# Transposing attention probabilities in row halves, and three moves in the order of VectorE and GpSimd

## The reference

```python
x = layernorm(x + self_attention(x))            # softmax(q k^T / 8) v per head, then w_o
x = layernorm(x + cross_attention(x, ctx))      # attends over heads within one position, not over positions
x = layernorm(x + light_ffn(x) + heavy_ffn(x))  # gelu FFNs 128->64->128 and 128->512->128 on rms-normed x
```

## Time and profile before

| what | us |
|---|---|
| median of 3 executions | 413.41 (412.16 to 416.49) |
| the profiled execution, its own time | 414.85 |
| its span, first to last instruction | 413.0 |
| PE busy / DVE busy / ACT busy / POOL busy | 398.8 / 287.6 / 240.1 / 148.1 |
| mean granted clock of TensorE | 0.994 |

### The profile page before, as it was taken

One profiled execution on the slowest core, in us unless ns is written; L12 is line 12 of the kernel. 1 busy time (PEld: TensorE's weight loads), 2 busy tenths in 40 slices (PEclk: granted clock), 3 DMA queues, 4 the chain that ended last, 5 costly groups with the idle time before them and its releaser, 6 DMA issues.

```text
span 413.0 us, 15941 instructions
## 1 busy us (share of the span) xinstructions
PE 398.8 (97%) x6580; PEld 344.6 (83%) x6580; DVE 287.6 (70%) x661; ACT 240.1 (58%) x813; POOL 148.1 (36%) x224
## 2 busy tenths in 40 slices
PE   8999999999999999999999999999999999798996
PEld 7787888788888888888888898888989888687884
DVE  4686786866848678667757868659566967578445
ACT  5675574745567466655566566457466648336351
POOL 0642434432413454323315444213324445123213
PEclk9999999999999999999999999999999999899999
DMA  7900113110110213100201112200201121102001
GB/s 262 356 5 8 44 26 83 46 32 9 33 23 19 45 32 87 41 14 8 42 13 32 37 41 75 51 2 17 44 8 39 27 49 22 33 12 43 27 26 52
DMA packets 43646, 19.27 MB, mean 47 GB/s; under 512 B 36592, under 2 KB 40944, under 8 KB 43584
## 3 DMA queue, kind: packets, MB, share of 16 engines
q1 hardware_dynamic: 42736, 16.88, 15.8%
q0 software_dynamic: 560, 1.38, 1.0%
q10 hardware_dynamic: 288, 0.07, 0.1%
HBM read 8.88 MB, written 1.05 MB: 24 GB/s over the span
## 4 chain that ended last, share of the span: by engine, by line
PE 83%; DVE 6%; ACT 4%; SPq 3%; issue 2%; DMA 1%; POOL 1%; POOLq 0%; DVEq 0%
PE ps L1151 8%; PE ps L1206 7%; PE ps L1139 7%; PE ps L1063 7%; PE ps L1118 6%; PE ps L1127 6%; PE ps L1035 6%; PE ps L1015 5%; PE ps L1017 4%; PE ps L1016 4%; PE ps L1161 4%; PE ps L1054 3%; SPq L309 3%; PE ps L1145 2%; ACT p L535 2%; PE ps L1094 2%
## 5 line engine op out<-in xcount | busy, mean ns | idle before, releaser
L535 ACT ACTIVATE p<-ps,neg_max 128x128 f32<-128x128 f32 x256 | 90.0, 383 | 42.9 <-DVE neg_max L799 42.9
L406 POOL TENSOR_TENSOR p<-p,row_inv 128x1024 f32<-128x1024 f32 x32 | 60.7, 1896 | 61.7 <-DVE row_inv L805 61.7
L528 ACT ACTIVATE pt<-ps 128x512 f32<-128x512 f32 x62 | 34.5, 625 | 48.7 <-PE ps L1118 48.7
L535 ACT ACTIVATION_READ_ACCUMULATOR p<-ps,neg_max 128x1 f32 x256 | 57.6, 225 | 0.0
L799 DVE TENSOR_REDUCE neg_max<-ps 128x4 f32<-128x512 f32 x64 | 41.5, 671 | 5.6 <-PE ps L1206 4.8
L745 DVE TENSOR_TENSOR ot<-ps,bv 128x512 f32<-128x512 f32 x32 | 22.0, 688 | 30.7 <-PE ps L1139 30.5
L1118 PE MATMUL ps<-ident,p 128*128 128x128 f32 x256 | 34.8, 279 | 1.3 <-POOL p L406 1.3
L1127 PE MATMUL ps<-x1t,wq 128*64 128x64 f32 x1024 | 34.0, 224 | 1.9 <-issue 1.0
L1206 PE MATMUL ps<-kt,qt 64*64 64x128 f32 x1024 | 35.1, 275 | 0.0
L1127 PEld LDWEIGHTS ps<-x1t,wq 128*64 128x64 f32 x1024 | 31.5, 138 | 3.5 <-issue 2.4
L1139 PEld LDWEIGHTS ps<-pt,v 128*64 128x64 f32 x512 | 28.9, 141 | 6.1 <-issue 6.1
(11 more groups left out here) (153 smaller groups left out, 838.1 us busy)
## 6 DMA issues: line engine op xcount, KB each, us to landing
v<-v2s SPq DMA_DIRECT2D x256, 32.0 KB
xg<-x_t SPq DMA_DIRECT2D x4, 256.0 KB, 3.0
pt<-w_qk SPq DMA_DIRECT2D x4, 256.0 KB, 5.1
cg<-ctx_t SPq DMA_DIRECT2D x4, 256.0 KB, 3.6
wo<-w_o SPq DMA_DIRECT2D x2, 512.0 KB, 9.2
xres<-x_nat SPq DMA_DIRECT2D x15, 64.0 KB, 1.7
out<-x2b SPq DMA_DIRECT2D x3, 256.0 KB, 2.3
p<-w_v SPq DMA_DIRECT2D x1, 512.0 KB, 7.0
```

The costliest lines, as they stand in the source:

```text
L406: nc.gpsimd.tensor_tensor(ph, ph, row_inv[:, 8 * half:8 * half + 8].unsqueeze(2).to_broadcast([T, 8, T]), ALU.mult).then_inc(p_ready, 1)
L528: nc.scalar.activation(pt[:, u * BANK:(u + 1) * BANK], bank(T_BANK[u]), ACT.Copy).then_inc(pt_ready, 1)
L535: last = nc.scalar.activation(p[:, hd * T:(hd + 1) * T], bank(S_BANK[q])[:, pos * T:(pos + 1) * T], ACT.Exp, bias=neg_max[:, hd:hd + 1], a ...
```

## The change

`transpose_p` now takes a half (8 heads). Per head it makes two transposes, of query rows 0 to 63 and of rows 64 to 127: a stationary operand of 64 rows by 128 columns and a 64x64 identity streamed through one row half of the array. The upper row half's output goes to one bank and the lower's to the other bank of the half. Both `mm_t` counts come at the end, behind head 7. ACT's copy has as many elements as before, and writes each bank as 8 pieces of 64 columns at a stride of 128 into `pt`. On DVE `inverse_sums(0)` moves from behind `x1_out` to between the two spreadings (or, in step 1, to ahead of `x1_out`), and `regrouped` moves from between the two `q2_out` to ahead of both. On POOL the first normalisation moves ahead of `x1_biased` (L381), to right behind the root.

```diff
+        def pt_part(u):
+            half, e = u // 2, u % 2
+            return (pt[:, half * 8 * T:(half + 1) * 8 * T].rearrange("p (h e q) -> p e h q", h=8, e=2)[:, e],
+                    bank(T_BANK[u]).rearrange("p (h q) -> p h q", h=8))
...
@@ POOL: rstd1 is split, its last part is x1_biased @@
+            def x1_biased(s, b_par):
                 if isinstance(s, int) and s == 1:
                     pool.wait_ge(in_bo2, 16)
                 pool.wait_ge(x1_ready, s)
...
@@ POOL: step; over_sum is the wait for inv_ready and the L406 product @@
-                for half in range(2):
-                    if a:
-                        pool.wait_ge(inv_ready, 2 * s + half + 1)
-                        ...
+                if a:
+                    over_sum(s, 0)
+                if bc:
+                    x1_biased(s, b_par)
+                if a:
+                    over_sum(s, 1)
...
@@ ACT: transposed(u), and the same in the tail @@
-                    nc.scalar.activation(pt[:, u * BANK:(u + 1) * BANK], bank(T_BANK[u]), ACT.Copy).then_inc(pt_ready, 1)
+                    dst, src = pt_part(u)
+                    nc.scalar.activation(dst, src, ACT.Copy).then_inc(pt_ready, 1)
...
@@ DVE: step @@
                     block_diagonal(s, 0)
+                if a and bc:
+                    inverse_sums(0)
+                if d:
                     block_diagonal(s, 1)
                 if bc:
                     x1_out(s)
...
                 if a:
-                    inverse_sums(0)
                     score_max(2)
...
-                    q2_out(s, 0)
                 if d:
                     regrouped(s)
                 if bc:
+                    q2_out(s, 0)
                     q2_out(s, 1)
...
@@ PE @@
-            def transpose_p(n, u):
-                if u % 2 == 0:
-                    pe.wait_ge(p_ready, 2 * n + u // 2 + 1)
-                for i in range(4):
-                    hd = 4 * u + i
-                    last = nc.tensor.transpose(bank(T_BANK[u])[:, i * T:(i + 1) * T], p[:, hd * T:(hd + 1) * T], ident[:])
-                last.then_inc(mm_t, 1)
+            def transpose_p(n, half):
+                pe.wait_ge(p_ready, 2 * n + half + 1)
+                for i in range(8):
+                    hd = 8 * half + i
+                    for e in range(2):
+                        rows = slice(HALF * e, HALF * e + HALF)
+                        mm = nc.tensor.transpose(bank(T_BANK[2 * half + e])[:, i * HALF:(i + 1) * HALF],
+                                                 p[rows, hd * T:(hd + 1) * T], ident[rows, rows])
+                        if i == 7:
+                            mm.then_inc(mm_t, 1)
...
-                    transpose_p(s - 1, 2)
-                    transpose_p(s - 1, 3)
+                    transpose_p(s - 1, 1)
...
                     transpose_p(s, 0)
-                    transpose_p(s, 1)
```

More of the change, by code:

```diff
@@ L387, in rms2, with over_sum @@
                 nc.gpsimd.tensor_tensor(x2b[:, bass.ds((s - 2) * D, D)], x2[:], bdl_row[:], ALU.add).then_inc(x2b_ready, 1)
+            def over_sum(s, half):
+                pool.wait_ge(inv_ready, 2 * s + half + 1)
+                ph = p[:, half * 8 * T:(half + 1) * 8 * T].rearrange("q (h k) -> q h k", h=8)
+                nc.gpsimd.tensor_tensor(ph, ph, row_inv[:, 8 * half:8 * half + 8].unsqueeze(2).to_broadcast([T, 8, T]),
+                                        ALU.mult).then_inc(p_ready, 1)
             def step(s, h, g, phase, a, bc, d):
@@ L400, in step @@
                     rstd1(s, b_par)
-                for half in range(2):
-                    if a:
-                        pool.wait_ge(inv_ready, 2 * s + half + 1)
-                        ph = p[:, half * 8 * T:(half + 1) * 8 * T].rearrange("q (h k) -> q h k", h=8)
-                        nc.gpsimd.tensor_tensor(ph, ph, row_inv[:, 8 * half:8 * half + 8].unsqueeze(2).to_broadcast([T, 8, T]),
-                                                ALU.mult).then_inc(p_ready, 1)
+                if a:
[4 more added lines that the diff above has]
+                    over_sum(s, 1)
                 if d:
@@ L422, in _ @@
             rstd1(B, 1)
+            x1_biased(B, 1)
             minus_max2(LAST)
@@ L1352, in _ @@
                 step(s, s // 2, s // GB, s % GB, s < B, 1 <= s <= B, s >= 2)
-            transpose_p(B - 1, 2)
-            transpose_p(B - 1, 3)
+            transpose_p(B - 1, 1)
             pe.wait_ge(wup_split, 2)
```

## The result

The changed kernel takes 431.21 us (median of 4, 429.78 to 432.15) beside 414.01 us (4, 412.16 to 416.49) for the kernel before: the ratio is 1.042, its 95% interval 1.037 to 1.046. It is 17 us slower where 3.6 us less were forecast. Its profiled execution took 432.15 us, with a span of 430.3. Many lines have new numbers: L1118 is now L1138, L771 is L788, L406 is L401, L1290 is L1311, L1063 is L1082.

The account below looks back on a forecast made before the run. PE, busy 97% of the span, was taken as the bound. Terms +9.0, -3.6, +1.2, -2.0, -1.0, +0.1 and +0.1 gave 3.8 us, taken as 3.6: 413.41 to 409.8 us, range 405.8 to 417.0.

Parts of the forecast that it names:

- its earlier start is worth nothing: POOL's first normalisation, moved ahead of the x1 bias: 1.3 us of spare in most steps, so no gain.
- DVE's reciprocal: Between the spreadings it waits for the last row sum; x1 comes 0.22 us late in nine steps, 2.0 us lost.
- the rivals: Pairs do not gain, 418.8 us (0.13); x1 not late, 407.1 (0.20); path moves off PE, 413.4 (0.15).
- A: Rival on PE's transposes: pairs take 0.109 us and do not gain, 418.8 us; decides from 0.080 a pair; chance 0.13.
- Transposes: On PE, a pair of half transposes takes 0.058 us against 0.109, saving 0.41 us per half on the path.
- The new change of layout: On PE, each half followed by a whole-array block pays 0.19 us; 19 halves, 3.6 us lost.
- The halves' sum: On PE, 22 halves save 9.0 us by shorter transposes, less 3.6 us for new layout changes.
- Regrouping and phase 3: Regrouping first on DVE gains 0.17 us in seven steps, 1.2; three phase 3 steps are 0.35 longer, 1.0 lost.

Follow-up runs that it names:

- the halves alone: Kernel before with only the transposes in row halves and ACT's copies, DVE and POOL in the old order: 411.27 us, ratio 0.994.
- regrouping kept back in phase 3: Kernel before plus halves and the regrouping first, except in phase 3, where it stays between both `q2_out`; reciprocal and POOL as before: 410.1 us, ratio 0.991.
- POOL's product back: Changed kernel with POOL's first normalisation again behind the x1 bias, all else of the change kept: 414.57 us, ratio 1.001 to the kernel before.
- the reciprocal back: Changed kernel with DVE's first reciprocal again behind `x1_out`, POOL keeping its new order: 409.04 us, ratio 0.989 to the kernel before.

## Why the prediction was wrong

**The step that failed** is "its earlier start is worth nothing", of POOL's move, with the `x1_out` of 0.34 us that the step "DVE's reciprocal" took over from the earlier trace rows ("`x1_out` at 236.64, its end 236.98"). Both steps looked at the edits one at a time, and one at a time both are right in kind: POOL's move alone costs nothing, the reciprocal's leaves `x1_out` at 0.34. I never laid the new start of POOL's product beside DVE's list. By the prediction's own figures the reciprocal ended near 236.1 and POOL was free right behind its root, so the product would run from about 236.2 to 238.1, over an `x1_out` at 236.64. The trace of before had the price of such a meeting, in the tail (L731, 0.62 us for 0.34), and I had not read it. Held to the end of the product, x1 would have been 1.4 us late instead of 0.2. Measured are 1.27 us a step, 17.8 us in 14 steps. None of the rivals held it; A, the slower one, stood for another mechanism, which did not come.

**Transposes: right.** A half takes 0.64 us in the chain. With the 0.15 of the earlier trace rows for the change of layout ahead of it a pair takes (0.64 - 0.15)/8 = 0.061 us, for 0.058 forecast. A's limit of 0.080 was not reached.

**The new change of layout: right.** The value projection behind a half takes 0.43 instead of 0.24 us, 0.19 as forecast, and `project_o2` 1.98 in every step but those of phase 3, where block A comes ahead of it and it keeps 1.78.

**The halves' sum: too high.** Forecast were 9.0 - 3.6 = 5.4 us. Between the kernel before and the halves alone, the stretches on PE from the start of a half to the next block shrink by 1.86 us (9 of them, each before a value projection), 1.68 (11, before `project_o2`), 1.14 (3, before L1035) and 0.72 (the rest), together 5.4. That this equals the forecast is chance: in the 1.68 are 1.6 us in which PE now waits for the regrouping. What I had not counted: the first records of the blocks behind are 0.4 us later, and from `project_q2` to the first half it is 1.51 us longer over 15 steps, not evenly but with single steps up to 0.9 longer or 0.8 shorter. The profile has 1.6 us of issue at `project_q2` where it had 1.0; the rest has no cause on record. Measured are 2.8 us by the medians, 2.9 at like clock, so about 0.6 us more stay open.

**Regrouping and phase 3.** The 7 x 0.17 = 1.2 us stand beside 0.75 measured alone, 1.8 at like clock. The chain of before has 1.96 us for `project_o2` also in steps 4 and 12, which the forecast did not count. In phase 3, PE waits 2.7 us ahead of block A in the three steps, but the 0.47 us that its second unit waited are gone. From the half's start to `project_o2` a step takes 4.56 us where it took 4.46: as forecast the half saves nothing there, and the step is 0.1 us longer, or 0.3 with x1's lateness, for 0.35. The run with the regrouping kept back in phase 3 has 4.46 again, so the order alone gives back only this 0.1.

**DVE's reciprocal: the size off.** 2.0 us were counted, for 9 steps and the small rest; measured are 3.3. The mechanism (it waits for the last sum, and the second spreading waits with it) and the delay of a step were right: in the trace with POOL's product back, against the one with the reciprocal back, PE reaches the transpose of x1 later by 2.38 us over 15 steps, and a further 0.5 us comes at the transposes behind. The number of steps was wrong: I had counted nine, and in the reciprocal's move alone the delay is 0.19 us in twelve steps and 0.07 in one.

## What to carry to other kernels

When an edit brings an instruction of GpSimd forward, write down its new interval and every VectorE instruction that begins inside it and works from SBUF to SBUF. A `tensor_scalar` that starts second may last until the other ends, here 1.6 us for 0.34; `bn_stats` was not held, and other instructions are to be looked up in the trace. The meeting may be in the trace already, as one slow member of a group: the longest time of a line beside its median shows it. Two moves that are each free can make such a meeting only together, so the intervals have to be drawn for the whole change, not edit by edit. The cures are cheap: let the short one start first, if only by 0.16 us, cut the long one into pieces, or give the short one an operand in PSUM.

## What the runs showed of the hardware that was not expected

**Hold between DVE and POOL**: a `tensor_scalar` from SBUF to SBUF that starts inside a product of POOL ends 0.08 us behind it, 1.59 against 0.34 us; a product in two pieces (2.04 instead of 1.90 us) lets it in between them; an operand in PSUM frees it (0.40 us). `bn_stats` in SBUF keeps its 0.29 us inside a product. How 0.3 us of work end 0.08 us behind the product's record, no run shows.

**TensorE's clock in the tail.** Behind step 15 PE waits 2.3 to 2.7 us for DVE ahead of the FFN products, and in some executions the granted clock then falls to 0.5 (1.2 GHz) for a time that differs from one execution to the next. The wait alone does not decide it: the third trace below has 2.7 us of it and keeps its clock, the first has 2.3. In three traces (stretch of the span: length, busy us and number of PE, PEld, DVE, ACT, POOL; the granted clock, then DMA), first of the kernel before:

```profile
350.00:354.00 4.00, 3.29 (x83) 2.86 (x81) 2.32 (x7) 1.68 (x4) 1.92 (x3) 1.00 0.24 52
354.00:358.00 4.00, 2.42 (x12) 1.61 (x14) 1.40 (x3) 1.81 (x3) 1.00 (x1) 0.83 0.23 51
358.00:362.00 4.00, 4.00 (x36) 3.61 (x33) 2.16 (x5) 1.15 (x2) 0.32 (x1) 0.74 0.00 0
```

of the run with POOL's product back:

```profile
350.00:354.00 4.00, 1.33 (x26) 1.12 (x19) 2.95 (x6) 1.33 (x3) 1.74 (x3) 0.82 0.23 49
354.00:358.00 4.00, 4.00 (x24) 3.06 (x24) 0.00 (x0) 2.72 (x4) 0.00 (x0) 0.50 0.17 37
358.00:362.00 4.00, 4.00 (x32) 3.57 (x31) 3.15 (x7) 0.60 (x1) 0.62 (x1) 0.83 0.00 0
```

and of the run with the reciprocal back, where the clock stays at full speed:

```profile
350.00:354.00 4.00, 2.78 (x28) 2.27 (x30) 1.11 (x4) 2.17 (x3) 1.00 (x1) 1.00 0.27 58
354.00:358.00 4.00, 4.00 (x37) 3.56 (x34) 3.73 (x10) 1.43 (x3) 0.69 (x2) 1.00 0.01 2
358.00:362.00 4.00, 3.85 (x85) 3.50 (x86) 2.89 (x7) 1.25 (x3) 2.10 (x5) 1.00 0.00 0
```

In the second, PE issues 24 matmuls in 4 us at 0.50, in the third 37 at 1.00. Between these two traces the two stretches of the tail around `weighted` differ by 2.8 us, of the 4.9 by which their spans differ. Over all kernels with executions of both kinds but those with a held `x1_out`, the executions with a mean clock below 0.997 are 1.3 to 3.6 us longer in the median than the others, for the kernel before 1.4 to 2.3. Effects of 1 or 2 us can be told in this kernel only with the clock beside them. What makes the clock fall in one execution and not in the next was not tried.
